# First loads in another order, the gates' tanh inside the first norm, and a query projection moved ahead of two transposes

## The reference

```python
x = x + jnp.tanh(g_xattn[0]) * _L0_xattn_ref(_layernorm(x, axis=-1), ctx_4096, wq, wk, wv, wo)
x = x + jnp.tanh(g_ffn[0])   * _L0_ffn_ref(_layernorm(x, axis=-1), W_q, scale, zero)
x = x + jnp.tanh(g_xattn[1]) * _L1_xattn_ref(_layernorm(x, axis=-1), ctx_4096, wq, wk, wv, wo, ln_w)
...
```

## Time and profile before

| | us |
|---|---|
| median of 3 runs | 1538.02 (1536.37 to 1538.24) |
| the profiled execution's own time | 1535.57 |
| its span, first to last instruction | 1533.8 |
| PE busy | 1370.0 (89%) |
| DVE busy | 1121.2 (73%) |
| ACT busy | 676.8 (44%) |

### The profile page before, as it was taken

How to read it: one execution, slowest core, us unless ns; L and a number is a source line. 1 busy time by engine, 2 the same in 40 slices (tenths; PEclk the granted TensorE clock), 3 DMA queues, 4 the chain that set the end, 5 groups by cost and what they waited for, 6 DMA issues and landing times.

```text
span 1533.8 us, 18726 instructions
## 1 busy us (share of the span) xinstructions
PE 1370.0 (89%) x6532; PEld 985.8 (64%) x6532; DVE 1121.2 (73%) x2045; ACT 676.8 (44%) x1403; POOL 336.4 (22%) x380
## 2 busy tenths in 40 slices
PE   6999999999997989987999998999999999999104
PEld 5665566566575658664788875777777777778102
DVE  4788898888888986946555567566566566667998
ACT  3777777777424434422222224444343443443104
POOL 1112112212163020321211111221212212122520
PEclk9999999999999989966999999999999999999557
DMA  5578988789710011512221310201101012000001
GB/s 214 151 170 185 238 219 198 172 212 221 209 42 1 1 56 34 106 35 49 49 69 54 102 69 1 69 28 43 43 27 69 28 42 69 1 1 1 0 0 56
DMA packets 37831, 127.76 MB, mean 83 GB/s; under 512 B 4928, under 2 KB 10944, under 8 KB 31536
## 3 DMA queue, kind: packets, MB, share of 16 engines
q1 hardware_dynamic: 26224, 83.38, 15.9%
q0 software_dynamic: 11520, 43.26, 14.8%
HBM read 72.63 MB, written 10.75 MB: 54 GB/s over the span
## 4 chain that ended last, share of the span: by engine, by line
PE 59%; DVE 22%; ACT 6%; DVEq 5%; DMA 4%; issue 2%; POOL 1%; SPq 1%; POOLq 0%
PE PS L150 12%; PE PS L152 11%; PE PS L151 11%; DVE AR L672 4%; PE PS L921 4%; PE PS L959 4%; DMA AR<-AR 3%; ACT s_sb L605 2%; DVE AR L2557 2%; PE PS L945 2%; DVE AR L2546 2%; DVE AR L2553 2%; DVEq L662 1%; DVE AR L678 1%; PE PS L266 1%
## 5 line engine op out<-in xcount | busy, mean ns | idle before, releaser
L436 POOL DMA_DIRECT2D AR<-AR x76 | 75.1, 1117 | 346.3 <-DMA AR<-AR 133.6
L151 PE MATMUL PS<-R16r 128*128 128x512 f32 (+1 forms) x328 | 122.1, 372 | 0.0
L508 PE MATMUL PS<-R,HT 128*128 128x256 f32 x512 | 116.5, 381 | 3.2 <-ACT R L594 2.7
L533 PE MATMUL PS<-R,PT 128*128 128x512 f32 x256 | 116.1, 596 | 3.4 <-DVE X L712 3.4
L152 PE MATMUL PS<-R16r 128*128 128x512 f32 (+1 forms) x312 | 119.1, 382 | 0.0
L508 PEld LDWEIGHTS PS<-R,HT 128*128 128x128 f32 x512 | 94.7, 190 | 16.2 <-ACT R L594 4.6
L1079 ACT COPY AR<-PS 128x512 f32<-128x512 f32 x64 | 37.5, 585 | 146.3 <-PE PS L152 145.8
L605 ACT ACTIVATE s_sb<-PS,sm 128x64 f32<-128x64 f32 x256 | 77.9, 336 | 53.1 <-DVE sm L697 52.6
L150 PE MATMUL PS<-HTr,R16r 128*128 128x512 f32 (+1 forms) x240 | 89.9, 374 | 3.0 <-DVE R16r L190 1.6
L150 PE MATMUL PS<-R16r,HTr 128*128 128x512 f32 (+1 forms) x224 | 90.2, 403 | 0.0
L152 PE MATMUL PS<-HTr,R16r 128*128 128x512 f32 (+1 forms) x240 | 87.4, 364 | 0.0
(11 more groups left out here) (311 smaller groups left out, 3574.7 us busy)
## 6 DMA issues: line engine op xcount, KB each, us to landing
AR<-AR POOLq DMA_DIRECT2D x76, 528.0 KB, 6.6
OR<-in_wo SPq DMA_DIRECT2D x12, 1024.0 KB, 12.2
dequantised<-AR SPq DMA_DIRECT2D x8, 1056.0 KB, 5.5
WR<-in_w0q SPq DMA_DIRECT2D x8, 1024.0 KB, 12.2
AR<-in_w3q SPq DMA_DIRECT2D x8, 1024.0 KB, 5.1
WR<-dequantised SPq DMA_DIRECT2D x22, 256.0 KB, 2.8
AR<-in_nf SPq DMA_DIRECT2D x4, 1056.0 KB, 9.3
nf_in<-in_nf SPq DMA_DIRECT2D x4, 1056.0 KB, 10.5
```

What stands on the lines that cost most here:

```text
L151: nc.tensor.matmul(out, ah, bl, start=False, stop=False)
L436: nc.gpsimd.dma_start(nf_below(g)[:, part], what[:, part], accum_op=ALU.add, max_dma_last_dim=4 * N_NF // 2).then_inc(added, 16)
L508: i = nc.tensor.matmul(bank(2 + u % 2)[:, tt * 256:(tt + 1) * 256], HT0[:, c, tok], m[:, :, c * B + b, :], start=c == 0, stop=c == C - 1)
L533: i = nc.tensor.matmul(bank(5 + tt), PT[:, at:at + P], vo[:, pr, b, :], start=pr == 0, stop=pr == 1)
```

## The change

There are three edits.

1. SP issues CT and WKV0 first, both counted on `kv_in`, then tiles 0 and 1 of X, then tiles 2 to 7 of X on a semaphore of their own, then WQ0 and the rest as before. DVE waits for the second part of X before the statistics of pair 1.
2. ACT's wait for the constants and its tanh stand after the pieces of the norm's tiles 2 and 3 and no longer first.
3. In a1, PE waits for the low parts of tiles 2 and 3 and does `project_q(1, 0)` ahead of the transposes of tiles 6 and 7.

```diff
-        x_in, consts_in, ctx_in = sem("x_in"), sem("consts_in"), sem("ctx_in")
+        x_in, x_rest_in, consts_in = sem("x_in"), sem("x_rest_in"), sem("consts_in")
...
             stat(0)
+            if n == 0:
+                dve.wait_ge(x_rest_in, 16)
             stat(1)
...
-                pe.wait_ge(A0["kv_in"], 16 * (g + 1))
+                pe.wait_ge(A0["kv_in"], 16 * (g + 2))
...
-            pe.wait_ge(ctx_in, 16)
             keys_values(0)
...
                     piece(0, k)
+                if t == 2:
+                    act.wait_ge(consts_in, CONSTS)
+                    nc.scalar.activation(tg[:], gates[:], ACT.Tanh).then_inc(gates_ready, 1)
...
             scores(0)
+            pe.wait_ge(lo_ready, T + 4)
+            project_q(1, 0)
             pe_norm_tile(pe, 2, 6)
             pe_norm_tile(pe, 2, 7)
-            project_q(1, 0)
             scores(1)
...
-            sp.dma_start(X[:], x_d.rearrange("(t p) n -> p t n", p=P)).then_inc(x_in, 16)
-            sp.dma_start(CT[:], ctxT_d).then_inc(ctx_in, 16)
+            x_tiles = x_d.rearrange("(t p) n -> p t n", p=P)
+            sp.dma_start(CT[:], ctxT_d).then_inc(A0["kv_in"], 16)
             sp.dma_start(WKV0, wkv_d[0]).then_inc(A0["kv_in"], 16)
+            sp.dma_start(X[:, 0:2], x_tiles[:, 0:2]).then_inc(x_in, 16)
+            sp.dma_start(X[:, 2:T], x_tiles[:, 2:T]).then_inc(x_rest_in, 16)
             sp.dma_start(WQ0, w0q_d[0]).then_inc(A0["q_in"], 16)
...
-            act.wait_ge(consts_in, CONSTS)
-            nc.scalar.activation(tg[:], gates[:], ACT.Tanh).then_inc(gates_ready, 1)
             act_x0(act)
```

## The result

The changed kernel took 1528.68 us, the median of 8 runs (1523.55 to 1533.1), where the kernel before took 1538.13 on the same chip (8 runs, 1535.78 to 1541.05). The ratio is 0.9948, with a 95% interval of 0.993 to 0.9965: 8.0 us less (5.4 to 10.8). The forecast was 6.6 less. The median of the eight runs lies 0.3 us under the range's lower end, 1529.0; 8.0 less than the 1538.02 that the forecast was made against is 1530.0, inside it. The profiled execution took 1528.6, with a span of 1526.9 against 1533.8: 6.9 less.

A forecast was written before the change was run, and what follows sets the result against it. The prediction took hand-overs between PE and DVE as the bound (59% and 22% of the last chain). Gains of 4.3 at the start and 2.3 in a1, 6.6 together, took 1538.02 to 1531.4 us; range 1529.0 to 1535.8.

The forecast's parts named there:

- The start's mechanism: At the start, earlier keys and norm let PE's first folded query begin at 15.2, not 19.48; gain 4.3 us.
- both edits of the start have one answer: At the start, the new load order and the later tanh go together, with one common gain of 4.3 us.
- The split's price: At the start, DVE's statistics of pair 1 wait for the rest of X, 12.1 for 11.19, 0.9 us later.
- loads in one queue don't each pay a start: At the start, queued transfers show no start of their own, so the rest of X comes at 12.1, not 14.1.
- a1: In a1, `project_q(1, 0)` fills PE's hole and `scores(1)` starts earlier; gain 2.3 us, nearer the fallen clock.
- Behind it DVE works almost without holes, so the gain carries: Behind a1's second score reduction, DVE has hardly any idle time, so the 2.3 us won there are kept.
- The sum: Over the whole kernel, 4.3 from the start plus 2.3 from a1 give 6.6 us less.
- Start lost in x0: In stage x0, longer DMA waits swallow the start's 4.3 us, leaving 2.3: 1535.7 us; chance 0.15.
- a1's gain does not come: In a1, the fallen clock makes `scores(2)` late for DVE; 4.3 and at best 1 remain: 1533.5 us; chance 0.15.
- Each load pays a start: At the start, about 1.2 us more for the rest of X; start gains 3.1, total 1532.6 us; chance 0.05.
- The clock stays full in a1: In a1, short holes don't lower PE's clock, so it gains 3.0 us: 1530.7 us; chance 0.2.
- Slower by one stretched DMA: In stage x0, one more accumulating DMA is stretched, 11.15 us over the median: 1542.6 us; chance 0.05.

The follow-up runs named there:

- start_only: The changed kernel with `project_q(1, 0)` back behind the transposes of tiles 6 and 7; 0.9972 of the kernel before, 4.3 us less (2.2 to 6.5).
- a1_only: The kernel before with only `project_q(1, 0)` moved ahead of the transposes of tiles 6 and 7; 0.9978, 3.4 us less (1.2 to 5.4).
- after_again: The changed kernel itself, unaltered, run once more in a later group on another chip; 0.9934 of the kernel before (0.9919 to 0.9948).
- after_warm: The changed kernel with 12 unread matmuls behind each of the transposes of tiles 6 and 7 in a1; 0.9977 of the kernel before.
- fill_hole: The changed kernel with `project_q(1, 1)` put between the transposes of tiles 6 and 7, ahead of `scores(1)`; 0.9979 of the kernel before.

## Why the prediction was right, point by point

- **The start's mechanism** was right in each link, and the term, 4.3, was 0.6 too small in the profile (4.9) and the same in the time of `start_only` (4.3), in part by luck, since the interval there is 2.2 to 6.5. The early links came 0.6 to 1.0 before their forecast, at 5.93 for 6.9, at 7.29 for 8.2 and at 11.47 for 12.1. I had timed all of them back from 12.10, the release behind the same 3072 KB in the old order; that these bytes are in 0.6 sooner now has no cause that a run shows. That the norm of tile 1 decides and not `kvs` held, though the keys took 6.41 and not 5.57.
- **That both edits of the start have one answer** was right, and more so than I said: alone, they give nothing that can be measured.
- **The split's price**, pair 1 behind the rest of X, was right in place and three times too large (0.9 later forecast, 0.28 measured: 11.47 for 11.19). That loads in one queue don't each pay a start: tiles 0 and 1 released DVE at 7.29, 1.4 behind WKV0, and the rest 4.2 later. The Trainium skill gives a fixed cost to each DMA in "DMA: Bandwidth & Descriptors", section "Anatomy of one DMA"; it doesn't say that loads in one queue pay it one after the other. Paid so, as the prediction's estimate had it, the rest of X would have come at 14.1 and the gain have been 2.3. These loads, issued by SyncE, don't show that.
- **a1.** `scores(1)` at the fallen clock (3.37; I took 3.78), the multiplication shortened by leaving POOL's split (1.50), and 2.2 won at the third reduction for the 2.3 of the sum: right, and by its two parts, 1.4 at the second reduction (forecast 1.1) and 0.8 by the shorter multiplication (forecast about 1). The weak step is "Behind it DVE works almost without holes, so the gain carries". It was read from one execution of the kernel before, in which DVE had no hole there. In two of four profiles of the old order another slow stretch follows that the new order has in none of five. The 3.4 of `a1_only` would fit a term made larger by it, and 4.3 + 3.4 = 7.7 would fit the 8.0 measured, but the interval of `a1_only` holds 2.3 as well, so that this is where the rest lies is likely and not shown.
- **The sum** was somewhat small. The result's interval, 5.4 to 10.8, holds the 6.6, and by it alone there would be nothing to explain; `after_again` gave 10.1 less (8.0 to 12.5), which leaves it out.
- **The range** had little to spare below. Its lower end was the sum of the upper bounds, 5.0 + 3.0, with 1 us for scatter. The start came to its bound in the profile (4.9), and a1's bound of 3.0 knew of one slow stretch only.
- **The rivals.** *Start lost in x0*: refuted by `start_only`. *a1's gain does not come*: refuted by `a1_only`, if narrowly, since the rival left at most 1 and the interval begins at 1.2. *Each load pays a start*: refuted by the releases above. *The clock stays full in a1*: it didn't (3.37). The rule that long gaps throttle the clock (the Trainium skill, "TensorE: Matmul & The Clock Gate", section "HAM oscillation") doesn't cover two short holes of 2.01 and 1.81, after which it stood at 0.72. Nor was the hole of 2.74, which the prediction took as agreeing with it, evidence that a long one is needed: in `start_only` the clock fell behind holes of 1.92 and 1.10, and in the kernel before, behind the same holes, it didn't. With the clock kept full at `scores(1)`, in `after_warm`, the third reduction came 2.4 earlier than before and not 3.0, since the multiplication ends with POOL's split, and the time rose. I had priced that case as the better one, and it is the worse; the part of the loss in a1 comes of that split, the rest is open. *Slower by one stretched DMA*: the changed kernel wasn't slower in either of its groups of runs.

**What stays open.** Behind a1 the lead of the changed kernel's profile over that of the kernel before moves up and down: 7.5 at the third reduction (482.37 - 474.83), 9.1 near 940 us, 7.4 soon after, 6.9 at the end. PE's timelines, before and then changed, of the same groups near 945 us:

```profile
949.24 1.08 PE L921 MATMUL PS<-OR,kvs 128*64 128x512 f32 x4 [3.06 <-DVE R16r L1213]
950.25 2.87 PE L959 MATMUL PS<-kT,AR 128*128 128x64 f32 x16
...
956.44 1.97 PE L921 MATMUL PS<-OR,kvs 128*64 128x512 f32 x4 [1.41 <-DVE R16r L1213]
```

```profile
940.17 1.97 PE L925 MATMUL PS<-OR,kvs 128*64 128x512 f32 x4 [3.06 <-DVE R16r L1217]
942.07 3.68 PE L963 MATMUL PS<-kT,AR 128*128 128x64 f32 x16
...
949.06 1.98 PE L925 MATMUL PS<-OR,kvs 128*64 128x512 f32 x4 [1.41 <-DVE R16r L1217]
```

The same hole of 3.06 stands ahead in both, but in the changed kernel the clock is down at once (1.97 for 1.08) and before only in the midst of the next group (2.87 for 3.68). The lead is 9.1 ahead of these groups and 7.4 behind them. It isn't the order of the work that decides this: `after_again`, a second profile of the changed kernel, has 1.08 and 2.96 there, as the kernel before has. Where the clock falls differs from execution to execution of one kernel, and I can't say beforehand which way; what decides it is open. Nor is the loss of the filled holes fully placed: against the changed kernel's profile, `fill_hole` is 7.8 longer, 2.4 of it ahead of a1's L190 pair, where the two kernels are the same, 2.1 in a1, and 3.3 behind. Only that of a1 is explained here.

## What to carry to other kernels

When two waits end within a microsecond of each other, take both away or neither: each edit alone measured as nothing here, together 4.3 us. Before paying work into a hole of TensorE, look at what slows behind the hole: the work moved was worth 2 to 4 us, 2.0 of them because it had run at the fallen clock, and filling further holes lost 3 to 7, of which 2 are explained: VectorE's multiplication could not end before GpSimd's split, so TensorE waited longer and its clock fell there. Before speeding up one engine, ask which other one's work, that doesn't move, will be the end of the same wait. Size a term that touches the clock from several executions of the kernel before, since a single one may lack a slow stretch that others have.

## What the runs showed that I had not expected

The scatter of this kernel's time goes with the clock. Over 27 runs of the kernel before, time and mean granted clock have a correlation of -0.91, from 1532.19 us at 0.943 to 1541.48 at 0.938; of the changed kernel's eight, the fastest, 1523.55, had 0.947 and the slowest, 1533.1, had 0.938. Two profiles of the same changed kernel show it in one place. The second is 0.7 us ahead of the first in its work here. The same window in the profile of the changed kernel and in that of `after_again`, and behind each a group of PE's timeline in it:

```profile
441.00:451.00 10.00, 8.00 (x49) 6.63 (x48) 9.37 (x19) 2.25 (x4) 8.07 (x11) 1.00 0.00 2
```

```profile
449.02 0.63 PE L268 MATMUL PS<-ident,HN 128*128 128x128 f32 x4 [0.60 <-DVE HN L206]
```

```profile
441.00:451.00 10.00, 8.00 (x42) 6.76 (x41) 9.44 (x20) 2.25 (x4) 7.60 (x12) 0.86 0.00 2
```

```profile
448.33 1.09 PE L268 MATMUL PS<-ident,HN 128*128 128x128 f32 x4 [0.60 <-DVE HN L206]
```

The holes ahead are the same, 1.40 and 0.60, and the clock is 1.00 in one window and 0.86 in the other, so that the same transposes take 0.63 and 1.09. (PE is busy 8.00 of 10.00 us in both, but with 49 and 42 matmuls: at the lower clock fewer fill the same time.) A profile shows one draw of this.

VectorE's multiplication of two SBUF operands (128x1024, f32) took 1.23 us alone and 1.50 to 3.03 when it began during GpSimd's subtraction of 4.5 us, by how much of that was left: each time it ended about 1.1 behind it. The profile puts the wait into the row's duration and shows no idle time for it.
